# Attention with a routed feed-forward layer: x arrives transposed for batches two to eight, and its normalisation is split over four engines

## The reference

```python
# x: (8, 224, 2048), ctx: (8, 750, 2048), all float32
x = x + attention(layernorm(x), ctx)      # softmax over ctx rows, no scaling, key = value = ctx
x = x + ffn(layernorm(x), ...)            # x @ W.T + b, plus a top-2 routed low-rank part of 16 experts

def layernorm(x): return (x - mean(x)) / sqrt(var(x) + 1e-5)    # over the last axis
def attention(q, k):
    a = einsum('bqd,bkd->bqk', q, k)
    return einsum('bqk,bkd->bqd', softmax(a), k)
```

## Time and profile before

| | |
|---|---|
| median of three runs | 1387.13 us |
| the three runs | 1379.29, 1387.13, 1390.94 us |
| the profiled execution, device time | 1381.78 us |
| its span, first to last instruction | 1380.0 us |
| granted TensorE clock, mean | 0.996 of full |
| PE busy | 1346.1 us (98%) |
| DVE busy | 937.2 us (68%) |
| ACT busy | 625.8 us (45%) |
| POOL busy | 310.3 us (22%) |

### The profile page before, as it was taken

One profiled execution on the slowest core, in us unless ns is written; L12 is line 12 of the kernel. 1 busy time (PEld: TensorE's weight loads), 2 busy tenths in 40 slices (PEclk: granted clock), 3 DMA queues, 4 the chain that ended last, 5 costly groups with the idle time before them and its releaser, 6 DMA issues.

```text
span 1380.0 us, 17969 instructions
## 1 busy us (share of the span) xinstructions
PE 1346.1 (98%) x6777; PEld 1104.9 (80%) x6777; DVE 937.2 (68%) x1193; ACT 625.8 (45%) x777; POOL 310.3 (22%) x233
## 2 busy tenths in 40 slices
PE   5999999999999999999999998999999999999998
PEld 4768888887878888786888886887888888888887
DVE  5577778778777878868556376777776664464644
ACT  3455655545555554555411366787785211111110
POOL 2001102020200202020614742445542111111110
PEclk9999999999999999999999999999999999999999
DMA  8967868787877868869756688999984978878785
GB/s 295 285 215 246 247 233 248 240 277 242 263 218 256 260 215 261 263 213 218 245 179 169 208 246 266 288 347 309 331 274 153 335 240 255 259 248 281 250 270 163
DMA packets 160248, 345.34 MB, mean 250 GB/s; under 512 B 51680, under 2 KB 68064, under 8 KB 145760
## 3 DMA queue, kind: packets, MB, share of 16 engines
q1 hardware_dynamic: 141600, 277.06, 64.8%
q0 software_dynamic: 10528, 52.85, 11.9%
q10 hardware_dynamic: 8064, 14.68, 3.0%
HBM read 260.87 MB, written 99.41 MB: 261 GB/s over the span
## 4 chain that ended last, share of the span: by engine, by line
PE 87%; DMA 7%; DVE 3%; issue 1%; ACT 1%; SPq 0%; POOL 0%; ACTq 0%; POOLq 0%; DVEq 0%
PE scores L887 13%; PE scores L889 13%; PE scores L888 13%; PE scores L753 6%; PE scores L755 6%; PE scores L754 6%; PE scores L856 6%; PE scores L858 6%; PE scores L857 6%; DMA y_scratch<-y_out,yrow_i 4%; PE work L790 3%; DMA x<-in_x_dram 2%; PE work L923 2%; PE work L924 2%; DMA w_in<-in_wT_dram 1%
## 5 line engine op out<-in xcount | busy, mean ns | idle before, releaser
L887 PE MATMUL scores<-w_h,a_h 128*128 128x512 f32 x896 | 351.9, 393 | 0.0
L889 PE MATMUL scores<-w_h,a_l 128*128 128x512 f32 x896 | 350.9, 392 | 0.0
L888 PE MATMUL scores<-w_l,a_h 128*128 128x512 f32 x896 | 350.4, 391 | 0.0
L1091 ACT ACTIVATE a_h<-a_in 128x512 fp32r<-128x512 f32 x148 | 83.6, 622 | 315.6 <-DMA a_in<-xT_scratch 213.0
L889 PEld LDWEIGHTS scores<-w_h,a_l 128*128 128x128 f32 x896 | 168.3, 188 | 37.8
L888 PEld LDWEIGHTS scores<-w_l,a_h 128*128 128x128 f32 x896 | 168.4, 188 | 37.0
L887 PEld LDWEIGHTS scores<-w_h,a_h 128*128 128x128 f32 x896 | 168.3, 188 | 36.9 <-DVE w_l L1461 0.2
L1470 DVE TENSOR_TENSOR a_l<-a_in,a_h 128x512 fp32r<-128x512 f32 x148 | 105.5, 759 | 123.3 <-ACT a_h L1091 119.6
L1223 DVE TENSOR_TENSOR raw_l<-raw_in,val_h 128x512 fp32r<-128x512 f32 x192 | 155.5, 827 | 47.5 <-ACT val_h L1017 46.7
L753 PE MATMUL scores<-ctxT_h,nT_h 128*112 128x494 f32 (+1 forms) x512 | 174.8, 341 | 1.1 <-DVE nT_l L1209 1.1
L755 PE MATMUL scores<-ctxT_h,nT_l 128*112 128x494 f32 (+1 forms) x512 | 172.2, 336 | 0.0
(11 more groups left out here) (150 smaller groups left out, 1990.7 us busy)
## 6 DMA issues: line engine op xcount, KB each, us to landing
ctxT_in<-in_ctxT_dram SPq DMA_DIRECT2D x64, 750.0 KB, 7.8
raw_in<-in_ctx_dram SPq DMA_DIRECT2D x32, 1280.0 KB
a_in<-xT_scratch SPq DMA_DIRECT2D x37, 1024.0 KB, 8.2
w_in<-in_wT_dram SPq DMA_DIRECT2D x32, 512.0 KB, 8.9
x<-in_x_dram SPq DMA_DIRECT2D x8, 1792.0 KB, 10.0
y_add<-y_scratch SPq DMA_DIRECT2D x56, 256.0 KB, 7.1
late_y<-y_scratch SPq DMA_DIRECT2D x56, 256.0 KB, 6.7
xn<-in_x_dram SPq DMA_DIRECT2D x7, 1792.0 KB, 15.3
```

Of the source, the lines that this page charges most:

```text
L887: pe.matmul(o, ah, wh, start=(k == 0), stop=False)
L888: pe.matmul(o, ah, wl, start=False, stop=False)
L889: last = pe.matmul(o, al, wh, start=False, stop=(k == KD - 1))
```

## The change

For batches two to eight the host gives x a second time, transposed (`xT`). PE no longer transposes x for them. SP loads the transposed x into the space of `nT_l`, under the name `xT_in`, behind the old batch's hidden part. The mean of each row is needed along the free axis there, the same on all partitions: POOL writes the small tile of means and variances to DRAM (`mean_d`), reads it back spread over all 128 partitions (`mean_in`, in the space of `bias_b`), and packs the means with one copy (`mean_b`). DVE subtracts it from the transposed x in four parts (`centre`), ACT makes the high parts (`x_high_part`) and DVE the low parts (`x_low_part`). The first two parts are done in the outputs (`CENTRE_AT`, `X_HIGH_AT`, `X_LOW_AT`), the other two in the scores of the next batch. The reciprocal root multiplies nothing ahead of the scores: ACT's exponential takes it as its scale, and DVE multiplies the row maximum with it in a second small instruction. ACT's two normalisations L1008 of `xn` go away.

The rows of x are loaded once for each batch instead of twice, alternately into `xn` and `x2`, behind the old batch's last transpose; the residual uses the same tile one batch later. The statistics of the next rows move from ahead of `eT` and blocks 4 and 5 to blocks 4 to 7, two instructions each (`STATS_AT`), the aggregate to block 8. In the first batch the load of x for the residual now stands ahead of three context loads. The middle batches are written out instead of looped, on all engines.

```diff
+STATS_AT = (4, 5, 6, 7)
+MEAN_AT = 8
+CENTRE_AT = (16, 18)
+X_HIGH_AT = (18, 20)
+X_LOW_AT = (19, 22)
...
+        rows = [xn, x2]
+        mean_in = bias_b[:, 0, 0:2 * LQ]
+        mean_b = bias_b[:, 1, 0:LQ]
...
                 if not last:
-
                     if first:
+                        load_row(1)
                         sp.wait_ge(filled, job_no("pre", 0, "qT", NX - 1) + 1)
-                    else:
-                        sp.wait_ge(filled, job_no("mid", b, "x2T", 0))
-                    sp.dma_start(xn[:, :, :], x_v[b + 1]).then_inc(xn_loaded, 16)
+                        sp.dma_start(xn[:, :, :], x_v[0]).then_inc(xres_loaded, 16)
                     for j in range(LR - 1):
                         score_done(sp, b, NPC - LR + j)
                         load_ctxT(b + 1, j)
                 if not first:
 
                     sp.wait_ge(filled, job_no(stage, b, "x2T", NX - 1) + 1)
-                sp.dma_start(x2[:, :, :], x_v[b]).then_inc(xres_loaded, 16)
                 if not last:
+                    if not first:
+                        load_row(b + 1)
                     score_done(sp, b, NPC - 1)
                     load_ctxT(b + 1, LR - 1)
+                    if not first:
+                        sp.wait_ge(filled, job_no(stage, b, "hid") + 1)
+                        sp.wait_ge(xT_staged, b * NX)
+                    load_xT(b + 1)
                     raw_again(b, 0)
...
                     pe.wait_ge(ctx_ready, b * NPC + j + 1)
-                    if stage == "first" and j % 2 == 0:
-                        pe.wait_ge(drained, job_no("pre", 0, "qT", j // 2) + 1)
+                    if j % 2 == 0:
+                        if stage == "first":
+                            pe.wait_ge(drained, job_no("pre", 0, "qT", j // 2) + 1)
+                        else:
+                            pe.wait_ge(x_ready, (b - 1) * NX + j // 2 + 1)
...
-                    if stage != "last" and e in QT_AT:
-                        pe.wait_ge(ln1_done, b * NQ + NQ)
-                        transpose_rows(stage, b, "qT", xn, QT_AT.index(e))
...
             def exponentials(b, q):
                 act.wait_ge(max_ready, b * NQ + q + 1)
                 act.activation(prob[:, q, 0:LK], all_scores(q), ACT.Exp, bias=nmax[:, q:q + 1],
-                               scale=1.0, accum_out=rsum[:, q:q + 1]).then_inc(exp_done, 1)
+                               scale=1.0 if b == 0 else rs1[:, q:q + 1],
+                               accum_out=rsum[:, q:q + 1]).then_inc(exp_done, 1)
+
+            def x_high_part(b, n):
+                act.wait_ge(centred, (b - 1) * NX + n + 1)
+                act.activation(four_blocks(nT_h, n), four_blocks(xT_in, n), ACT.Copy).then_inc(x_high, 1)
 
             def one(b, stage):
                 for j in range(HR, NPC):
                     ctx_high(b, j)
+                    if stage != "first" and j in (3, 5):
+                        x_high_part(b, 2 + (j - 3) // 2)
...
+                dve.reduce_max(nraw[:, q:q + 1], all_scores(q), AX.X, negate=True).then_inc(max_step, 1)
+                dve.wait_ge(rstd1, b + 1)
+                dve.wait_ge(max_step, (b - 1) * NQ + q + 1)
+                dve.tensor_tensor(nmax[:, q:q + 1], nraw[:, q:q + 1], rs1[:, q:q + 1],
+                                  ALU.mult).then_inc(max_ready, 1)
+
+            def centre(b, n):
+
+                if n == 0:
+                    dve.wait_ge(xT_loaded, b * 16)
+                    dve.wait_ge(mean_ready, b)
+                cut = slice(4 * n, 4 * n + 4)
+                dve.tensor_tensor(xT_in[:, cut, :], xT_in[:, cut, :],
+                                  mean_b.unsqueeze(1).to_broadcast([P, 4, LQ]), ALU.subtract).then_inc(centred, 1)
+
+            def x_low_part(b, n):
+                dve.wait_ge(x_high, (b - 1) * NX + n + 1)
+                dve.tensor_tensor(four_blocks(nT_l, n), four_blocks(xT_in, n), as_f32(four_blocks(nT_h, n)),
+                                  ALU.subtract).then_inc(x_ready, 1)
...
+            def spread_mean(b):
+
+                pool.wait_ge(aggr1, b * NQ + NQ)
+                pool.dma_start(mean_d[b], mv1[:, :, :]).then_inc(mean_stored, 16)
+                pool.wait_ge(mean_stored, b * 16)
+                pool.dma_start(mean_in, mean_d[b].rearrange("p q s -> (p q s)").unsqueeze(0).to_broadcast([P, 2 * LQ])
+                               ).then_inc(mean_loaded, 16)
+                pool.wait_ge(mean_loaded, b * 16)
+                at_least(pool, centred, (b - 1) * NX)
+                pool.tensor_copy(mean_b.rearrange("a (q p) -> a q p", q=NQ),
+                                 mean_in.rearrange("a (p q s) -> a q p s", q=NQ, s=2)[:, :, :, 0]
+                                 ).then_inc(mean_ready, 1)
...
+            spread_mean(1)
             for b in range(1, NB - 1):
                 reciprocal_root(ve2, rs2, var2, rstd2, b - 1)
                 stage_xT("mid", b, b - 1)
                 reciprocal_root(ve1, rs1, var1, rstd1, b + 1)
+                spread_mean(b + 1)
```

More of the change, by code:

```diff
@@ L62, in build_identity, with xattn_ffn_kernel @@
                        pattern=[[-1, P]], channel_multiplier=1).then_inc(sem, 1)
-def xattn_ffn_kernel(nc, x, ctx, bias, ctxT, arT, wT, bT, out):
+def xattn_ffn_kernel(nc, x, ctx, bias, ctxT, xT, arT, wT, bT, out):
     NB, LQ, D = x.shape
@@ L162, in xattn_ffn_kernel @@
         "pre": group("qT", NX),
-        "first": group("eT", NQ) + group("qT", NX),
-        "mid": BEFORE + group("eT", NQ) + OLD + group("qT", NX),
+        "first": group("eT", NQ),
+        "mid": BEFORE + group("eT", NQ) + OLD,
         "last": BEFORE + group("eT", NQ) + OLD,
@@ L358, in xattn_ffn_kernel @@
         x_first = [sem(f"x_first{c}") for c in range(CH)]
-        xn_loaded = sem("xn_loaded")
+        row_loaded = [sem(f"row_loaded{i}") for i in range(2)]
+        xT_loaded = sem("xT_loaded")
+        mean_stored = sem("mean_stored")
+        mean_loaded = sem("mean_loaded")
+        mean_ready = sem("mean_ready")
+        centred = sem("centred")
+        x_high = sem("x_high")
+        x_ready = sem("x_ready")
+        max_step = sem("max_step")
         xres_loaded = sem("xres_loaded")
@@ L679, in _ @@
             sp.wait_ge(fresh_stored, 16)
+            sp.wait_ge(centred, (NB - 1) * NX)
             load_bias(0)
@@ L949, in _ @@
             one(0, "first")
-            with pe.Fori(1, NB - 1) as b:
+            for b in range(1, NB - 1):
                 one(b, "mid")
@@ L1121, in _ @@
             one(0, "first")
-            with act.Fori(1, NB - 1) as b:
+            for b in range(1, NB - 1):
                 one(b, "mid")
@@ L1390, in one @@
                             dve.wait_ge(x2_done, b * (NQ * CH))
-                        for i in range(4 * j, 4 * j + 4):
-                            stats(x2, st2, stat2, i)
-                        if j == 1:
-                            dve.wait_ge(stat2, b * (NQ * CH))
+                        for i in range(0, 5) if j == 0 else (5,):
+                            stats(rows[(b - 1) % 2], st2, stat2, i)
                     if old and j == 2:
+                        for i in (6, 7):
+                            stats(rows[(b - 1) % 2], st2, stat2, i)
+                        dve.wait_ge(stat2, b * (NQ * CH))
                         aggregate(st2, mv2, aggr2)
                         variance(mv2, ve2, aggr2, var2, b - 1)
+                    if old and j in (2, 4):
+                        centre(b, 2 + (j - 2) // 2)
+                    if old and j in (3, 5):
+                        x_low_part(b, 2 + (j - 3) // 2)
                     if stage == "first" and j == 3:
@@ L1413, in one @@
                     x2T_low(NX - 1)
-                if new and old:
-                    dve.wait_ge(xn_loaded, b * 16 + 16)
-                    for i in range(4):
-                        stats(xn, st1, stat1, i)
                 for q in range(NQ):
@@ L1425, in one @@
                     c, t = e // NT, e % NT
[L1426 to L1433 removed]
+                    if new and e in STATS_AT:
+                        n = STATS_AT.index(e)
+                        if n == 0:
+                            dve.wait_ge(row_loaded[(b + 1) % 2], (b + 2) // 2 * 16)
+                        for i in range(2 * n, 2 * n + 2):
+                            stats(rows[(b + 1) % 2], st1, stat1, i)
+                    if new and e == MEAN_AT:
+                        dve.wait_ge(stat1, (b + 2) * (NQ * CH))
                         aggregate(st1, mv1, aggr1)
                         variance(mv1, ve1, aggr1, var1, b + 1)
[L1436 to L1437 removed]
+                    if new and e in CENTRE_AT:
+                        centre(b + 1, CENTRE_AT.index(e))
+                    if new and e in X_LOW_AT:
+                        x_low_part(b + 1, X_LOW_AT.index(e))
                     if old and e == HN_AT + 3:
@@ L1443, in one @@
                         tile_low(0, (FIRST_A_AT.index(e),))
```

(5 more changed lines are left out.)

82 lines of the change are left out of this document (37 added, 45 removed).

## The result

The changed kernel takes 1397.88 us (median of 13 runs, 1392.13 to 1402.18). In runs taken beside them the kernel before takes 1381.04 us (13 runs, 1377.64 to 1390.94). The ratio is 1.01, with an interval from 1.0081 to 1.012; the medians over all runs are 16.8 us apart. The profiled execution took 1395.97 us, with a span of 1393.9 us. The change makes the kernel slower by about 1%, where a gain of 1.3% was forecast.

A forecast was written before the change was run, and what follows sets the result against it. PE was taken as the bound, busy 480.00 of 480 us in the six whole batches. Terms -19.6 - 4.5 + 0.7 + 3.6 + 1.5 + 0.7 = -17.6 us gave 1364.2 us profiled, median 1369.5 us, range 1357 to 1392 us.

The forecast's parts named there:

- the mean's way over DRAM: Outputs, ahead of block 17: mean packed at 406.1 us, needed by 405.5; 0.6 us late, 3.6 us lost in six batches.
- slower rival: Ahead of block 17: landings of 5.7 and 6.7 us, PE stalls 3.8 us plus 1.7 low clock; 1402.9 us, chance 0.12.
- the Trainium skill: Mean's store and load: 2.0 us plus bytes over 436e3 gives 2.0 and 2.5 us, mean ready at 401.3, no wait.
- the full gain: Outputs, ahead of block 17: mean ready before 405.5 us, no stall; 22.7 us gained, 1364.4 us, chance 0.15.
- Transposes: PE in the outputs: 28 groups of eight transposes of xn go, 0.70 us each, 19.6 us gained.
- Early load of x in the first batch: First batch's outputs: residual load ahead of three context loads saves 2.8 us of PE standstill and 1.7 of slow clock, 4.5 us.
- Transposed x late in the first batch: First batch's outputs: transposed x lands at 84.2 us, DVE asks at 82.5; late by nothing to 1.7, 1.5 us lost.
- Exponential and scores together: Second row-maximum instruction delays ACT's exponential; statistics and subtraction delay the context's fourth low part; 0.7 us lost each, seven batches.
- Statistics: Outputs, blocks 4 to 7: DVE falls back but keeps 0.3 us of room; nothing lost, upper end 1 us in six batches.
- DVE at 86% as the bound: Statistics and scores: both at their upper ends, 6 and 9.8 us, make DVE the bound; 1384.6 us, chance 0.10.
- a distance of batches of 77.3 us: Sign in PE's rows: distance from batch to batch should fall from 79.3 to some 77.3 us.
- PE's wait ahead of block 17: Sign of the mean's landing, for DVE's low part: 0.6 us each by forecast, otherwise none, 2.0 or 3.8.

The follow-up runs named there:

- the quiet trip: Changed kernel with one more SP wait, holding the next values' load and all behind it until the mean has landed; 1377.94 us, ratio 0.9966.
- the kernel without a trip: Changed kernel without the mean's DRAM store and load; POOL packs zeros instead, so the result is not the reference's; 1361.44 us, ratio 0.9833.

## Why the prediction was wrong

**The step that failed** is the one on the mean's way over DRAM, and in it the size of the two landings. The prediction took 4.3 us for the store, the middle between the shortest landing of a small store (3.3) and a scatter (5.3), and 4.9 us for the load, the shortest landing of the bias, "since the longer ones lay behind other transfers on SP's queue and POOL's queue is empty then". The runs show 5.9 and 6.6 us. With them the step that was put at 3.6 us cost 39.7. An empty queue says nothing: the transfers of all queues share the DMA engines, and these are full at just that time. The two experiments that settle it are the quiet trip (same queue, few other transfers: 1.7 and 3.5 us) and the trip on ACT's queue (other queue, same transfers: 5.7 and 5.4 us). The medians of the earlier trace rows, 5.7 and 6.7 us, were the right rows, and the prediction had them in its slower rival: mean packed at +17.4 us from block 6, a stall of 3.8 us and 1.7 us of low clock in each of seven batches, 38.5 us. It was 17.0 us in batch five, and over all seven 3.6 us of stall and 2.1 us besides, 39.7 us. That rival's 1402.9 us, with a chance of 0.12, is 5 us above the measured time; as a loss it is 15.8 us (38.5 less 22.7) against 16.8 measured. Its mechanism was right and its sizes nearly so. The mistake was to argue away the one set of rows that came from this kernel under its usual load.

The sum of that step in batch five, from the start of ACT's block 6 (391.91 in the earlier trace rows, 402.61 after), in us:

| | predicted | measured |
|---|---|---|
| root ends | 3.6 | 4.4 |
| store and the gaps around it | 4.6 | 6.2 |
| load | 5.0 | 5.9 |
| copy | 1.0 | 0.6 |
| packed | 14.2 | 17.0 |
| latest time without a stall | 13.6 | 14.0 |

The root is 0.8 us later, since the rows of x landed 10.0 us after their issue and DVE waited 0.99 us for them, where the prediction had taken no wait. The copy was over-sized (0.56 us, not 1.0), and without a stall block 17 would have started 0.4 us later than eleven blocks behind block 6, since PE lost 0.7 us ahead of blocks 8 and 10. These nearly cancel. The store and the load are 2.5 of the 2.8 us of difference; and a stall of 3 us then brings the low clock with it, which the forecast's 0.6 us would not have.

The sentence on **the Trainium skill** (DMA: Bandwidth & Descriptors, Anatomy of one DMA — SWDGE (gpsimd) path) is borne out in part: by 2.0 us plus bytes over 436e3, the estimate was 2.0 and 2.5 us (which makes the mean ready at 401.4 us, not 401.3). With quiet engines 1.7 and 3.5 us are measured. In the kernel as changed, it is 5.9 and 6.6 us; the measurement decides, and the full gain that hung on that rule didn't come.

**The other terms**, tested by the kernel without a trip. It starts the eighth batch's outputs 21.9 us earlier than before; the prediction's terms without the mean's 3.6 us give 21.2.
- Transposes, 19.6 us: right. In six middle batches the outputs are 36.73 less 33.82 = 2.91 us shorter, against four groups by 0.70 us.
- Early load of x in the first batch, 4.5 us: 42.06 less 35.13 less 2.8 for the transposes there, 4.1 us, though 1.6 us of low clock at the start of that stage, which the kernel before did not have, stand against it. The size is right within what one profile tells of a first batch.
- Transposed x late in the first batch, 1.5 us: it wasn't. In the kernel without a trip DVE subtracts at 82.51 us, the time that the prediction had for its asking, with no wait for the load in the list. This term was wrong.
- Exponential and scores together, 1.4 us in seven batches, 0.2 each: 42.90 less 42.60 is 0.3 us each.
- Statistics, put at nothing: nearly right. PE waits a little for DVE between blocks 7 and 10, about where the prediction had placed the sign of a DVE that is the bound. It loses 2.4 us by it in four batches of the kernel after, and 1.0 us in two batches of the one without a trip.
- DVE at 86% as the bound: no, as above.

As signs in the profile the prediction had named a distance of batches of 77.3 us (it is 82.3 = 39.43 + 42.9, and 76.7 without the trip), PE's wait ahead of block 17 with a granted clock below 1.00 for the long ones, and DVE's wait for x in the first batch gone. The last two came true, the wait ahead of block 17 in the form that it had given to the slower rival.

## What to carry to other kernels

A small transfer in the middle of a busy stage lands late: price it by the landings of small transfers under the same load (here some 6 us, twice in a row), also if the queue that issues it is empty, and not by what it would take alone. If a few hundred numbers must go from rows to all partitions, a broadcast copy and a transpose on PE did it for 0.4 us of PE per batch, where the way over DRAM took 13 us and had to be hidden. A forecast by a margin of 0.6 us on a path of 14 us is a forecast of either sign, above all where a gap of 3 us costs PE's clock as well.

## What was unexpected of the hardware

- Holding back other transfers, with a single wait on SP, made the same two transfers 3.5 and 1.9 times as fast (5.9 to 1.7 us, 6.6 to 3.5 us).
- The low clock is a large part of the price of a gap: 12.7 to 14.7 of 39.7 us. Behind the gap of 3.17 us in the first batch the granted clock was 0.50 for the next 3.05 us, behind that of 5.77 us 0.50 for 4.47 us. But the length of a gap alone doesn't settle it. In the kernel after, the gap of 3.06 us in batch two was followed by 1.00 and the shorter ones of 2.89 and 2.73 us by 0.62 and 0.65 for 4.5 us. In the quiet trip the 2.70 us behind a gap of 3.05 us ran at 1.00, and the 4.92 us behind a gap of 2.05 us at 0.65. No run shows what decides it. The windows of that kernel (columns as above):

```profile
269.80:272.50 2.70, 2.68 (x15) 2.28 (x16) 1.57 (x2) 2.70 (x4) 0.00 (x0) 1.00 0.98 368
...
433.98:438.90 4.92, 4.92 (x19) 4.15 (x20) 3.67 (x3) 3.40 (x5) 0.00 (x0) 0.65 1.00 377
```

- A one-column operation of DVE took 1.27 us instead of 0.16 while POOL made its sum of 2x896 columns (387.65 us, 2.12 us long) beside it. DVE's timeline in the scores of batch five:

```profile
386.41 0.16 DVE L1278 TENSOR_TENSOR nmax<-nraw,rs 112x1 f32<-112x1 f32 x1
...
388.52 1.27 DVE L1278 TENSOR_TENSOR nmax<-nraw,rs 112x1 f32<-112x1 f32 x1
```

The second ends at 389.79, as POOL's ends at 389.77. It is so in each of the seven batches: 0.16 us for the first half of the query, 1.25 to 1.27 for the second, with POOL's sum beside it each time. Why stays open. Scores to outputs take 0.3 us longer in all than before; the prediction had this step at 0.2 us.
